# One over the deviation in the last phase: a square root and a reciprocal, or a logarithm and an exponential from one table set

## What is computed

```python
def _layernorm(x, axis=-1, eps=1e-05):
    m = jnp.mean(x, axis=axis, keepdims=True)
    v = jnp.var(x, axis=axis, keepdims=True)
    return (x - m) / jnp.sqrt(v + eps)

# attention: q, k, v = x @ Wq, x @ Wk, x @ Wv, split into heads
scores = jnp.einsum('bhqd,bhkd->bhqk', q, k) * HEAD ** (-0.5)
scores = jnp.where(causal, scores, -jnp.inf)
weights = jax.nn.softmax(scores, axis=-1)
out = jnp.einsum('bhqk,bhkd->bhqd', weights, v)      # heads joined, @ Wo + bo

# quantised product
lhs_scale = _absmax_scale(lhs, (2,))                 # max|.| / 127, per row
rhs_scale = _absmax_scale(rhs, (0,))                 # per column
q_lhs = jnp.clip(jnp.round(lhs / lhs_scale), -127, 127).astype(jnp.int8)
q_rhs = ...
acc = jax.lax.dot_general(q_lhs, q_rhs, ...)

x = x + attention(_layernorm(x))
x = x + quantised_product(_layernorm(x), L0_ffn_rhs)
```

## Time and profile before

| | us |
|---|---|
| median of three executions | 1724.77 |
| lowest and highest | 1723.46, 1725.1 |
| the profiled execution | 1728.75 |
| its span, first to last instruction | 1727.0 |
| PE busy | 1628.2 (94%) |
| DVE busy | 1529.3 (89%) |
| ACT busy | 1362.9 (79%) |
| POOL busy | 311.9 (18%) |

### The profile page before, as it was taken

The page is one execution under the profiler, slowest core; times in us unless marked ns, Lnnn a source line. Parts: engine busy times, 40 slices in busy tenths (PEclk is TensorE's granted clock), DMA queues, the critical chain, the costliest instruction groups (busy, mean ns, idle before and its releaser), DMA issues.

```text
span 1727.0 us, 39723 instructions
## 1 busy us (share of the span) xinstructions
PE 1628.2 (94%) x16319; PEld 639.8 (37%) x16319; DVE 1529.3 (89%) x1825; ACT 1362.9 (79%) x2622; POOL 311.9 (18%) x366
## 2 busy tenths in 40 slices
PE   6999999999999999999999999999999999998864
PEld 4455443333333333333333333333333333343433
DVE  4777769999999999999999999999999999476777
ACT  2333349999999999999999999999998998787852
POOL 5333310101111111111110101011111111333330
PEclk9999999999999999999999999999999999998976
DMA  3443320101010111111111111010101160146432
GB/s 112 142 136 118 110 74 17 48 18 49 18 49 18 49 30 36 34 33 33 32 42 38 36 34 48 18 49 18 49 18 49 54 157 15 50 125 180 132 112 79
DMA packets 103497, 106.14 MB, mean 61 GB/s; under 512 B 20112, under 2 KB 86932, under 8 KB 103316
## 3 DMA queue, kind: packets, MB, share of 16 engines
q1 hardware_dynamic: 103316, 103.60, 20.5%
HBM read 60.52 MB, written 42.47 MB: 60 GB/s over the span
## 4 chain that ended last, share of the span: by engine, by line
PE 60%; DVE 18%; ACT 3%; DMA 2%; issue 1%; SPq 1%; POOL 0%; ACTq 0%; DVEq 0%; POOLq 0%
PE psum L1006 28%; PE psum L987 12%; DVE pmax L352 12%; PE psum L260 10%; PE psum L274 3%; PE psum L279 3%; DVE pblk L352 2%; PE psum L1043 2%; ACT prob L1167 1%; DMA V<-ust 1%; DMA unnormalised<-ust 1%; DVE V L1296 1%; PE psum L1067 1%; ACT L1140 1%; DVE V L1273 1%
## 5 line engine op out<-in xcount | busy, mean ns | idle before, releaser
L1167 ACT ACTIVATE prob<-psum 128x512 f32<-128x512 f32 (+1 forms) x2304 | 1181.7, 574 | 143.9 <-PE psum L987 120.7
L352 DVE TENSOR_REDUCE pmax<-psum 128x2 f32<-128x1024 f32 (+1 forms) x960 | 1107.4, 1216 | 25.4 <-PE psum L260 11.5
L1006 PE MATMUL psum<-prob,V 128*32 128x256 f32 x8704 | 690.5, 394 | 0.0
L987 PE MATMUL psum<-Q,K 50*128 50x512 f16 (+3 forms) x2560 | 466.2, 351 | 8.8 <-ACT prob L1167 7.4
L1212 POOL TENSOR_SCALAR_AFFINE_SELECT prob<-prob 128x512 f32<-128x512 f32 x256 | 159.5, 635 | 1153.9 <-ACT prob L1167 1152.5
L260 PE MATMUL psum<-K,Q 48*128 48x512 f16 x1536 | 300.0, 387 | 15.6 <-DVE pmax L352 15.6
L1006 PEld LDWEIGHTS psum<-prob,V 128*32 128x32 f32 x8704 | 177.7, 109 | 289.2 <-issue 237.8
L987 PEld LDWEIGHTS psum<-Q,K 50*128 50x128 f16 x2560 | 183.8, 94 | 219.9 <-ACT prob L1167 136.4
L260 PEld LDWEIGHTS psum<-K,Q 48*128 48x128 f16 x1536 | 74.4, 93 | 309.5 <-DVE pmax L352 188.9
L352 DVE TENSOR_REDUCE pblk<-psum 128x8 f32<-128x1024 f32 x128 | 152.2, 1217 | 2.1 <-PE psum L279 1.1
L279 PE MATMUL psum<-K,Q 48*128 48x512 f16 (+3 forms) x1024 | 128.8, 299 | 0.0
(11 more groups left out here) (107 smaller groups left out, 733.4 us busy)
## 6 DMA issues: line engine op xcount, KB each, us to landing
f_x<-in_L_attn_x SPq DMA_DIRECT2D x32, 512.0 KB, 3.8
unnormalised<-ust SPq DMA_DIRECT2D x64, 256.0 KB, 3.1
q_parts<-part SPq DMA_DIRECT2D x64, 128.0 KB
k_parts<-part SPq DMA_DIRECT2D x64, 128.0 KB
Q<-q_parts SPq DMA_DIRECT2D x128, 64.0 KB, 2.3
K<-k_parts SPq DMA_DIRECT2D x128, 64.0 KB, 2.1
out<-V SPq DMA_DIRECT2D x16, 512.0 KB, 3.6
f_us<-unnormalised SPq DMA_DIRECT2D x28, 256.0 KB
```

The costliest lines, as they stand in the source:

```text
L352: nc.vector.tensor_reduce(to, of, axis=AX.X, op=ALU.max).then_inc(M.mx_free, 1)
L987: m = nc.tensor.matmul(PS[:, SB + i % RING, at:at + n], K[it % 2][rows, pair, kb * P:(kb + 1) * P], Q[it % 2][rows, pair, (c + 1) * CH - n ...
L1006: m = nc.tensor.matmul(PS[32 * h:32 * h + 32, UB, to:to + n], V[:, it // NG * NT + kb, col:col + 32], prob[(it * NSTEP + k) % PRING][:, h, ...
L1167: nc.scalar.activation(prob[g % PRING][:, h, 0:n], PS[:, SB + i % RING, 0:n], ACT.Exp, scale=by).then_inc(exp_done, 1)
```

## The change

The square root on ACT and the reciprocal on DVE are replaced by two activations on ACT: the logarithm of variance plus epsilon, and the exponential of minus a half times that, which is one over the deviation. Logarithm and exponential are both in the table set `natural_log_exp_and_others`, and the kernel asks for that set ahead of the attention, where before it ran a small exponential. The logarithm stands where the square root stood, in unit 2; the exponential stands in unit 3, ahead of `take_hT`. In the periods behind the attention ACT's order of units is 0, 1, 2, 3 instead of 0, 1, 3, 2. DVE waits for `rstd_ready` from ACT directly.

```diff
@@ project
-        table = sb("table", [P, 1])
...
-                    nc.scalar.activation(table[:], eps[:], ACT.Exp)
+                    nc.scalar.preload_act_table_set("natural_log_exp_and_others")
@@ attend, ACT
-            def deviation(j):
+            def log_of_variance(j):
                 act.wait_ge(var_ready, j + 1)
-                nc.scalar.activation(std[j % 2], mv[j % 2][:, :, 1], ACT.Sqrt, bias=eps[:, 0:1]).then_inc(std_ready, 1)
+                nc.scalar.activation(logvar[j % 2], mv[j % 2][:, :, 1], ACT.Ln, bias=eps[:, 0:1]).then_inc(log_ready, 1)
+
+            def one_over_std(j):
+                act.wait_ge(log_ready, j + 1)
+                nc.scalar.activation(rstd[j % 4][:], logvar[j % 2], ACT.Exp, scale=-0.5).then_inc(rstd_ready, 1)
 
             def unit(p, u):
                 if u in (0, 1) and 0 <= p - 2 < NC:
                     over_scale(p - 2, u)
                 if u == 2 and 0 <= p - 1 < NC:
-                    deviation(p - 1)
+                    log_of_variance(p - 1)
+                if u == 3 and 0 <= p - 1 < NC:
+                    one_over_std(p - 1)
                 if u == 3 and 0 <= p - DELAY < NC:
                     take_hT(p - DELAY)
...
             for p in range(UNDER, PERIODS):
-                for u in (0, 1, 3, 2):
+                for u in (0, 1, 2, 3):
                     unit(p, u)
@@ attend, DVE
-            def one_over_std(j):
-                dve.wait_ge(std_ready, j + 1)
-                nc.vector.reciprocal(rstd[j % 4][:], std[j % 2]).then_inc(rstd_ready, 1)
-
...
                 if p - 1 < NC:
-                    one_over_std(p - 1)
                     normalise(p - 1)
```

More of the change, by code:

```diff
@@ L822, in attend @@
         mv = [in_values([TPC, 2]) for s in range(2)]
-        std = [in_values([1, TPC])[:, 0, :] for s in range(2)]
+        logvar = [in_values([1, TPC])[:, 0, :] for s in range(2)]
         rstd, amax, rowscale, rowinv = ([sb(f"f_{name}{s}", [P, TPC]) for s in range(4)] for name in
@@ L834, in attend @@
         var_ready = sem("f_var_ready")
-        std_ready = sem("f_std_ready")
+        log_ready = sem("f_log_ready")
         rstd_ready = sem("f_rstd_ready")
```

## The result

The kernel after takes 1736.82 us (median of 4 runs, 1733.94 to 1740.92), the kernel before on the same chip 1724.93 (1723.46 to 1725.57): a ratio of 1.0071, interval [1.005, 1.0092], 11.9 us more. Forecast were 1719.7 us and a range of 1714 to 1728. The sign was wrong, and the time lies outside the range.

The account below looks back on a forecast made before the run. PE was taken to set the pace under the attention, DVE's queue in the tail. Attention 8.1 us earlier (7.8 - 1.4 + 0.9 + 1.5 - 0.7), tail +3.0: 5.1 less, 1719.7 us on the median, range 1714 to 1728.

Parts of the forecast that it names:

- What goes: ACT loses 27 table loads, 34.6 us, and gains 16 exponentials, 4.8 us: 30 us lighter; DVE loses 2.8 us of reciprocals.
- The gain from it: Under the attention, PE's waits shrink, so the attention ends 8.1 us earlier, the sum of five terms.
- the four that belong to the loads: PE's waits for ACT gone 7.8; swallowed by DVE chains -1.4; first chain sooner 0.9; one wait for add of x 1.5.
- One over the deviation may come later ... I take 0.7: Under the attention, the exponential behind another exponential pair: five of ten places later, 2.6 us together; 0.7 us counted as loss.
- The first lateness: At the first load under the attention, one over the deviation ready at 1504.0 against DVE's start at 1503.54.
- Loss in the tail: Behind the attention, hT(12)'s copy stands behind logarithm and exponential, PE idles and its clock drops: 3.2 us lost, 3.0 net.
- Rival 1: The tail loses nothing because PE keeps or regains its clock: 8.1 us less, 1716.7 us; chance 0.19.
- Rival 2: DVE's add of x becomes PE's wait in most periods; some 3 us come through and the tail takes them: 1724.8; chance 0.23.
- Rival 3: Slower: DVE sets the pace, late one over the deviation costs all 2.6 us, gain 0, tail 3.2: 1730.6 us; chance 0.13.

Follow-up runs that it names:

- experiment 3: Kernel after with logarithm and exponential both in unit 2 under the attention and the old unit order (0, 1, 3, 2) in the tail: 1718.59 us, 0.9956 of before.
- experiment 4: Kernel after with only the tail's old unit order put back, exponential still in unit 3 under the attention: 1736.22 us, 1.0059 of before.
- experiment 8: Kernel after with the tail's old order, exponential in unit 3 under the attention, and GpSimd's divide waiting for DVE's add of x: 1713.91 us, 0.9929 of before.
- experiment 7: Kernel after with both activations in unit 2 under the attention, old tail order, divide behind the add of x: 1711.7 us, 0.991 of before; again 1713.19, 0.9934.
- experiment 1: Kernel after with only GpSimd's divide waiting for DVE's add of x instead of PE's projection: 1716.86 us, 0.9951 of before.
- 2: Kernel before (square root and loads) with only GpSimd's divide waiting for DVE's add of x: 1723.78 us, 0.9989 of before.

## Why the prediction was wrong, point by point

- **What goes: right.** ACT has 32.5 us less, forecast 30. Log 301 ns and exponential 206, taken 0.30 each. PE's waits for ACT fell from 6.8 to 0.6.
- **The gain from it: right in size, taken back.** Of the attention's terms the four that belong to the loads (7.8 - 1.4 + 0.9 + 1.5) make 8.8, and the nearest to a reading of them alone is experiment 3: 7.6 us (the interval gives 5.2 to 10.0, and the reciprocals are in it).
- **"One over the deviation may come later ... I take 0.7": the step that failed.** It measured 17.8 us (experiment 3 against 4). The first lateness itself was worked out well (0.46 at chunk 0, measured 0.31); what it sets off was not. The term had no collision with GpSimd in it: with the divide behind the add of x the same step measures 0.0019 or less (experiment 8 against 7), some 3 us at most by the medians and inside the intervals, so the 0.7 isn't refuted for the lateness by itself. First, I laid the new ACT order against PE's times of the trace before, as if those stood still. PE's next scores stand behind the bias matmul that waits for DVE, so DVE's delay returns to DVE through PE and ACT, and with more idle time PE's clock fell too (0.88 granted from 0.94). Second, I never placed GpSimd's divide. It was hidden before, 0.47 us clear of the row scale, and the faster PE brought it 0.77 forward.
- **Loss in the tail: right for the order of units.** After its wait the copy of hT(12) begins at 1705.68, straight behind logarithm and exponential:

```profile
1705.24 0.30 ACT L1139 ACTIVATE V<-V,eps 128x4 f32<-128x4 f32 x1 [7.98 <-DVE V L1291]
1705.57 0.20 ACT L1143 ACTIVATE f_rstd<-V 128x4 f32<-128x4 f32 x1
1705.68 0.99 ACT L1134 COPY V<-psum 128x1024 bf16<-128x1024 bf16 x1
```

  and PE answers (beside the earlier trace rows):

```profile
1706.73 1.89 PE L1066 MATMUL psum<-f_wq,V 128*128 128x256 bf16 x8 [4.29 <-ACT V L1134]
1708.55 0.60 PE L1040 MATMUL psum<-f_bo,f_ones 3*128 3x512 bf16 x1
1709.08 3.78 PE L1042 MATMUL psum<-f_wo,V 128*128 128x256 f32 x8
```

  4.29 us of wait instead of 1.10, the product 1.89 (I had 1.9), and the last add of x waits 3.21 for PE (I had 3). From the last copy of sums to the end the traces take 58.0 after and 55.1 in experiment 4, and 57.6 in experiment 1 against 55.7 in 8: 2.9 and 1.9 for the order alone, forecast 3.0. By the medians 0.0012 and 0.0022, 2 to 4 us, neither clear of its intervals. Against before (56.4) the tail is only 1.6 longer: in the old order (experiment 4) it is 1.3 shorter than before, of which I had 0.2 for a reciprocal; where the rest comes from stays open.
- **Rival 1** fell: in the traces the tail loses. **Rival 2** had the right wait, but as one that merely swallows the gain. **Rival 3** named the place, DVE's normalisation behind the late exponential with PE at the bias matmul, and the sign, but priced it at the sum of first delays, 5.8, and got 0.13. The argument against it (PE busy 95%, DVE 67%) is a share of busy time, and says nothing of three engines that wait for each other in a ring.
- The last sentence of the prediction said it is wrong "if the waits for DVE grow by what those for ACT lose". They grew by 12.8, more than the 7.8 (6.8 + 1.0) that those for ACT lost.

Open: how the 17.8 us divide between the held row scale, the waits that it sets off and the clock; why unit 1 brings nothing more; and whether 7 and 8 differ at all.

## What to carry to other kernels

Splitting a dependent pair of steps around queued work is a change of its own: price it apart from what the steps save (here -7.6 us for the loads, +17.8 for the split, and nearly nothing for the split once the divide was out of the way). Where engines wait for each other in a ring, don't judge a delay on fixed times of the old trace, and place every GpSimd instruction that a faster engine releases earlier: what it will stand beside on DVE decides. A cheap first look at such a change is the mean duration of instructions it doesn't touch; one that grew many times over names the neighbour.

## What the runs showed of the hardware

A VectorE instruction over 128x4 numbers, 0.17 us when free, took 1.94 and 1.95 us behind a GpSimd tensor_tensor of 2.36 us and ended with it; behind one of 1.25 us it took 0.85. The normalisation (tensor_scalar over SBUF) is held too (mean 740 ns from 469), while beside the same divide the add of x out of PSUM took 1.16 us and the maximum (TENSOR_REDUCE at 1518.80, into which the divide of 1519.61 fell) its usual 1.22. The Trainium skill (SBUF — State Buffer, SBUF: two separate sides) says that GpSimd and VectorE share a port pair as an exclusive lock, held for the whole instruction, and that only some VectorE instructions want it. The runs agree, down to the halves, and they give the price that matters: not the size of the instruction held, but the rest of the one that holds.

27 table loads of 1.283 us gone, and 16 short exponentials come, took 32.5 us off ACT but only 7.6 us off the time, or 9.5 to 13.6 with the divide later (experiment 7 beside 2).
